# A low-pass filter between two channel projections: images unrolled, first and second matmuls side by side, the corner term moved to VectorE

## The reference

```python
xs = jnp.einsum('bhwc,dc->bhwd', x, W1) + b1      # x: (16, 64, 64, 768) f32, W1: (192, 768)
xs = jax.nn.gelu(xs, approximate=False)
xs = fft_low(xs)       # per image and channel: keep the 32 x 32 low frequencies of the 64 x 64 FFT, then abs()
xs = jnp.einsum('bhwd,cd->bhwc', xs, W2) + b2     # back to 768 channels
return x + xs
```

## Time and profile before

| | |
|---|---|
| median of 3 runs | 2668.43 us (2667.24 to 2670.11) |
| profiled execution, span from the first to the last instruction | 2680.7 us |
| own time of the profiled execution | not listed; its span stands 12.3 us (0.46%) over the median |
| mean granted TensorE clock | 0.975 of full speed |
| TensorE busy | 95% |
| DMA, mean of 16 engines | 59.8% of the span, 509 MB |

### The profile page before, as it was taken

The page is one execution under the profiler, slowest core; times in us unless marked ns, Lnnn a source line. Parts: engine busy times, 40 slices in busy tenths (PEclk is TensorE's granted clock), DMA queues, the critical chain, the costliest instruction groups (busy, mean ns, idle before and its releaser), DMA issues.

```text
span 2680.7 us, 53277 instructions
## 1 busy us (share of the span) xinstructions
PE 2549.4 (95%) x16864; PEld 2485.4 (93%) x16864; DVE 1833.9 (68%) x3980; ACT 1350.4 (50%) x3077; POOL 397.9 (15%) x500
## 2 busy tenths in 40 slices
PE   8899898998999989899998999989999899998999
PEld 7799898998989989899898999989999899998999
DVE  6487575775758757587675766757667576675767
ACT  5355454554545545455454545545455454554544
POOL 1102021020211202112020120201202012020120
PEclk9899999999999999999999999999999999999999
DMA  6474664746647466474665846558455584555845
GB/s 207 106 252 138 201 242 114 264 129 200 240 114 261 131 198 242 114 273 129 204 230 129 282 116 215 208 135 298 103 211 202 140 300 99 207 204 145 299 102 221
DMA packets 342566, 509.48 MB, mean 190 GB/s; under 512 B 78418, under 2 KB 210770, under 8 KB 342228
## 3 DMA queue, kind: packets, MB, share of 16 engines
q1 hardware_dynamic: 342228, 505.31, 59.8%
HBM read 253.60 MB, written 251.66 MB: 188 GB/s over the span
## 4 chain that ended last, share of the span: by engine, by line
PE 83%; DMA 6%; SPq 4%; issue 3%; DVE 2%; ACT 2%; DVEq 0%; ACTq 0%
PE ps L400 22%; PE ps L385 12%; PE ps L401 10%; PE ps L472 6%; PE ps L462 6%; PE ps L463 5%; PE ps L469 5%; PE ps L466 5%; DMA xt_hi<-filtered_rows 4%; PE ps L437 3%; SPq L317 2%; PE ps L411 2%; PE ps L445 2%; DMA filtered_rows<-filt 2%; PE ps L413 2%
## 5 line engine op out<-in xcount | busy, mean ns | idle before, releaser
L400 PE MATMUL ps<-w1s,xt_hi 128*128 128x384 f32 x3072 | 980.2, 374 | 0.0
L521 ACT ACTIVATE xt_hi<-ps 128x512 fp32r<-128x512 f32 x768 | 457.7, 598 | 697.8 <-PE ps L385 674.5
L401 PE MATMUL ps<-w1s,xt_lo 128*128 128x192 f32 x3072 | 772.3, 251 | 0.0
L640 DVE TENSOR_TENSOR xt_lo<-ps,xt_hi 128x512 fp32r<-128x512 f32 x768 | 529.8, 691 | 282.4 <-ACT xt_hi L521 279.6
L702 DVE TENSOR_TENSOR xs<-ps,xs 128x384 f32<-128x384 f32 x1024 | 564.5, 556 | 210.9 <-PE ps L472 159.8
L401 PEld LDWEIGHTS ps<-w1s,xt_lo 128*128 128x128 f32 x3072 | 588.0, 191 | 0.0
L400 PEld LDWEIGHTS ps<-w1s,xt_hi 128*128 128x128 f32 x3072 | 578.8, 188 | 0.0
L472 PE MATMUL ps<-w2b_hi,ob 128*128 128x384 f32 x1024 | 357.0, 349 | 42.7 <-DVE ob L693 42.7
L763 POOL TENSOR_TENSOR diff<-hid 128x192 f32<-128x192 f32 x240 | 232.2, 967 | 1016.8 <-ACT hid L529 1016.8
L462 PE MATMUL ps<-w2a_hi,oa_hi 128*128 128x384 f32 x1024 | 361.3, 353 | 20.8 <-DVE xs L702 19.7
L385 PE MATMUL ps<-ident,xs 128*128 128x128 f32 x2304 | 344.1, 273 | 11.2 <-DMA xs<-x_dram 10.6
(11 more groups left out here) (62 smaller groups left out, 3051.3 us busy)
## 6 DMA issues: line engine op xcount, KB each, us to landing
out_dram<-xs SPq DMA_DIRECT2D x127, 1536.0 KB, 9.3
xs<-x_dram SPq DMA_DIRECT2D x80, 1536.0 KB, 7.2
filtered_rows<-filt SPq DMA_DIRECT2D x256, 192.0 KB, 2.0
x_tail<-x_dram SPq DMA_DIRECT2D x32, 1536.0 KB, 8.5
xs<-x_dram SPq DMA_DIRECT2D x32, 768.0 KB, 6.3
xt_hi<-filtered_rows SPq DMA_DIRECT2D x64, 256.0 KB, 5.1
cols_b<-filtered_rows SPq DMA_DIRECT2D x128, 128.0 KB, 5.4
xt_lo<-filtered_rows SPq DMA_DIRECT2D x64, 256.0 KB, 6.4
```

The lines of the kernel that those rows point to most:

```text
L400: nc.tensor.matmul(ps_h[t % 2][:, 0:2 * D], hi, w1s[:, k, :], start=k == 0, stop=False)
L401: ins = nc.tensor.matmul(ps_h[t % 2][:, D:2 * D], lo, w1s[:, k, 0:D], start=False, stop=k == KC - 1)
L521: nc.scalar.activation(xt_hi[:, n % XT_SLOTS, :], ps_xt[n % 2][:], ACT.Copy).then_inc(s_xhi, 1)
L640: nc.vector.tensor_tensor(xt_lo[:, n % XT_SLOTS, :], ps_xt[n % 2][:], xt_hi[:, n % XT_SLOTS, :].bitcast(F32), ALU.subtract).then_inc(s_xlo, 1)
```

## The change

The image loop is gone: all 256 pairs (ALL) of the 16 images are unrolled in one list of steps. Step s has first matmuls of pair s and second matmuls of pair s - 17 (LAG = 17). The filter along H of image i stands in step 16 i + 17, after the first unit of that step, so one step after `filter_w_pair` of the image's last pair. In that step the four halves of the second matmuls come at the end.

`xs` becomes 18 slots of a pair. Three of four pairs are kept in 16 slots from their transposes to their store. Every fourth pair is loaded once for the transposes and once more for the addition (`load_again`), each into one slot of its own. Loads and stores are of one pair (768 KB) instead of four tiles. The copy by ScalarE (565) goes.

`filtered_rows` becomes two tensors, `rows_a` (128 channels) and `rows_b` (64), each pair written with two DMAs. They are read back in five groups of four DMAs as pairs become ready: pairs 0 to 3, 4 to 7, 8 to 11, 12 to 14, and pair 15 alone. A group of n pairs goes to 4 n partitions for each half of W, with contiguous runs of 16 KB or 8 KB. `cols_a` has its own memory.

The corner is no longer 12 matmuls. `corner_values` makes 64 columns with two small float32 matmuls, VectorE copies them (`corner_copy`), and adds them while it stores each of the 12 banks (`y_group`), so that VectorE stores all 12. ScalarE then takes the absolute value in place (`y_group_positive`). The banks rotate over four (`ps_y`). Identity and W1 are loaded by ScalarE's queue.

```diff
-LAG = 8
+LAG = PAIRS + 1
+READS = [(0, 4), (4, 4), (8, 4), (12, 3), (15, 1)]
...
+            def write_rows(p):
+                i, q = divmod(p, PAIRS)
+                sp.wait_ge(s_fs, p + 1)
+                if q == 0 and i > 0:
+                    sp.wait_ge(s_cols, 16 * READ_DMAS * i)
+                sp.dma_start(rows_in[0][:, 2 * q:2 * q + 2, :], filt[:, p % 2, :, 0:P]).then_inc(s_rw[p % 2], 16)
+                sp.dma_start(rows_in[1][:, 2 * q:2 * q + 2, :], filt[:, p % 2, :, P:D]).then_inc(s_rw[p % 2], 16)
+            def read_rows(i, n):
+                first, number = READS[n]
+                end = i * PAIRS + first + number
+                sp.wait_ge(s_rw[0], 32 * ((end + 1) // 2))
+                sp.wait_ge(s_rw[1], 32 * (end // 2))
...
+                h = slice(4 * first, 4 * (first + number))
                 for w2 in range(2):
+                    sp.dma_start(cols_a[w2 * H + h.start:w2 * H + h.stop, :, :],
+                                 rows_a[h, w2 * W2:(w2 + 1) * W2, :]).then_inc(s_cols, 16)
+                    sp.dma_start(cols_b[w2 * H + h.start:w2 * H + h.stop, :, :].rearrange("p m n -> p (m n)"),
+                                 rows_b[h, w2 * W2:(w2 + 1) * W2, :].rearrange("h w d -> h (w d)")).then_inc(s_cols, 16)
...
+            for s in range(STEPS + 1):
+                if s + 2 < ALL:
+                    load_first(s + 2)
+                if 0 <= s - LAG - 1 < ALL - 1:
+                    store(s - LAG - 1)
+                if 1 <= s <= ALL:
+                    i, q = divmod(s - 1, PAIRS)
+                    for n, (first, number) in enumerate(READS):
+                        if first + number == q:
+                            read_rows(i, n)
+                    write_rows(s - 1)
+                    if q == PAIRS - 1:
+                        read_rows(i, len(READS) - 1)
+                p = s - LAG + 2
+                if 0 <= p < ALL and again(p):
+                    load_again(p)
...
+            def corner_values(i):
+                pe.wait_ge(s_twice, i + 1)
+                pe.wait_ge(s_fs, PAIRS * (i + 1))
+                nc.tensor.matmul(ps_f[:, 2 * D:2 * D + 32], corner_acc[:, 0:P], kmat[:], start=True, stop=True)
+                nc.tensor.matmul(ps_f[:, 2 * D + 32:2 * D + 64], corner_acc[:, P:2 * P], kmat[:], start=True, stop=True).then_inc(s_cmm, 1)
+            def filter_h(i):
+                pe.wait_ge(s_cols, 16 * READ_DMAS * (i + 1))
+                pe.wait_ge(s_add, HALVES * i)
+                for g in range(GROUPS):
...
+                    if g == 3:
+                        pe.wait_ge(s_corner, i + 1)
+                    elif g >= 4:
+                        pe.wait_ge(s_yev, GROUPS * i + g - 3)
                     for m in range(4):
...
+                        ins = nc.tensor.matmul(bank[:, m * P:(m + 1) * P], data, fh[:], start=True, stop=True)
                     ins.then_inc(s_y, 1)
...
+            for s in range(STEPS):            # TensorE
+                i, r = y_image(s), second_pair(s)
+                for j in range(UPP):
+                    if UPP * s + j + AHEAD < UNITS:
+                        transpose_unit(UPP * s + j + AHEAD)
+                    if s < ALL:
+                        mm1_unit(UPP * s + j)
+                    if j == 0 and i is not None:
+                        corner_values(i)
+                        filter_h(i)
+                    if j == 1 and 1 <= s <= ALL:
+                        filter_w_pair(s - 1)
+                    if r is not None and i is None:
+                        for u in OUT_HALVES[j]:
+                            out_half(r, u)
+                if i is not None:
+                    for u in range(4):
+                        out_half(r, u)
...
+            def y_group(i, g):                # VectorE
...
+                fix = corner[:, g % 3 // 2, :].rearrange("p (n m) -> p n m", m=4).unsqueeze(1).to_broadcast([P, 16, 8, 4])
+                nc.vector.tensor_tensor(y_of_group(g).rearrange("p (r n) m -> p r n m", n=8),
+                                        ps_y[g % 4][:].rearrange("p (m r n) -> p r n m", m=4, n=8), fix,
+                                        ALU.add).then_inc(s_yev, 1)
...
+            def y_group_positive(i, g):       # ScalarE
+                act.wait_ge(s_yev, GROUPS * i + g + 1)
+                y = y_of_group(g)
+                nc.scalar.activation(y, y, ACT.Abs).then_inc(s_yab, 1)
```

More of the change, by code:

```diff
@@ L353, in _, with load_first @@
-            turns(sp, turn)
-            for g in range(MAIN_GROUPS):
-                sp.wait_ge(s_out[g], 16 * IMAGES)
-            sp.wait_ge(s_tail_out, 16 * (TAIL_GROUPS * IMAGES + GROUP - 1) + 1)
-            for n in range(2):
-                sp.wait_ge(s_fw[n], 16 * PAIRS // 2 * IMAGES)
+            def load_first(p):
+                slot = slot_first(p)
+                if again(p) and nth_use(p) > 1:
+                    sp.wait_ge(s_t, UPP * (p - 4) + UPP)
+                elif not again(p) and nth_use(p) > 1:
+                    sp.wait_ge(s_st[slot], 16 * (nth_use(p) - 1))
+                elif slot in (12, 13, 14):
+                    sp.wait_ge(s_setup, SET_UP)
+                if p == 0:
+                    sp.dma_start(xs[:, 0:1, :], x_v[:, 0:1, :]).then_inc(s_x_first, 16)
+                    sp.dma_start(xs[:, 1:2, :], x_v[:, 1:2, :]).then_inc(s_ld[0], 16)
+                else:
+                    sp.dma_start(x_pair(slot), x_v[:, 2 * p:2 * p + 2, :]).then_inc(s_ld[slot], 16)
@@ L361, in _ @@
+            store_last_pair()
+            for slot in range(SLOTS):
+                stored = sum(16 for p in range(ALL) if slot_second(p) == slot)
+                if slot == slot_second(ALL - 1):
+                    stored += 16
+                if stored:
+                    sp.wait_ge(s_st[slot], stored)
         @block.tensor
@@ new lines, in _ @@
+            for n in range(AHEAD):
+                transpose_unit(n)
+            for s in range(STEPS):
[16 more added lines that the diff above has]
+                        out_half(r, u)
@@ L593, in _ @@
-            turns(act, turn)
+            for n in range(AHEAD):
+                xt_hi_unit(n)
+            for s in range(STEPS):
+                i, r = y_image(s), second_pair(s)
+                for j in range(UPP):
+                    if UPP * s + j + AHEAD < UNITS:
+                        xt_hi_unit(UPP * s + j + AHEAD)
+                    if j == 0 and 1 <= s <= ALL:
+                        gelu_pair(s - 1)
+                    if j == 0 and i is not None:
+                        for g in range(GROUPS):
+                            y_group_positive(i, g)
+                        split_hi_pair(r)
+                    if j == 2 and 1 <= s <= ALL:
+                        stage_filtered(s - 1)
+                    if r is not None and j == (0 if i is None else 2) and r + 1 < ALL and not image_starts(r + 1):
+                        split_hi_pair(r + 1)
+                    if j == 2 and s in (2, 3):
+                        set_up_hi(s - 2)
@@ L610, in set_up_filters @@
             def set_up_filters():
[L611 to L612 removed]
+                dve.wait_ge(s_const, 16 * CONSTANTS)
                 link(nc.vector.tensor_copy(fw_hi[:], fwf))
@@ L745, in _ @@
-            turns(dve, turn)
+                slot = slot_second(p)
+                dve.wait_ge(s_o, n + 1)
+                if u == 0 and again(p):
+                    dve.wait_ge(s_ld[AGAIN_C], 16 * nth_use(p))
+                x_half = xs[:, 2 * slot + t, f * HALF:(f + 1) * HALF]
+                nc.vector.tensor_tensor(x_half, ps_o[n % 3][:, 0:HALF], x_half, ALU.add).then_inc(s_add, 1)
+            set_up_at = {0: set_up_filters, 1: set_up_w2, 4: set_up_w2a_lo, 5: set_up_w2b_lo,
+                         6: set_up_b2_hi, 7: set_up_b2_lo, 8: set_up_b2_lo_rest}
```

709 lines of the change are left out of this document (262 added, 447 removed).

## The result

The changed kernel takes 2768.9 us (median of 4 runs, 2762.3 to 2771.4) beside 2667.8 us for the kernel before on the same chip: a ratio of 1.037 (95% interval 1.034 to 1.040), slower by 3.7%. I had forecast 2612 us and a range that ended at 2675 us. The profiled execution has a span of 2764.6 us at a mean granted clock of 0.951.

A forecast was written before the change was run, and what follows sets the result against it. TensorE, busy for 95% of the span, was taken as the bound. Terms 2247.7 + 158.4 + 148.8 + 24 + 33.5 + 12 gave 2624.4 us of span, 2612 us at the median; range 2535 to 2675 us.

The forecast's parts named there:

- Side by side everywhere: First and second matmuls paired in all steps: 256 pairs at 8.78 us, 2247.7 us, with every fourth pair's second load hidden.
- The wait for the reads: TensorE waits ahead of the filter along H for the last filtered rows: 9.05 us per image, 148.8 us in all.
- The rival on the other side: Read rate goes by partition count: wait of 18 us, 2756 us, 3.3% slower; chance 0.12 for waits above 12 us.
- The corner: Filter along H: twelve 0.32 us matmuls per image go, banks take 0.80 us at TensorE's pace; 158.4 us in all.
- the account against before: Changes from the old span: corner -61, old stalls and slow clock -198, new wait, clock and stall +206, start and end -7.
- The slow clock: After the wait for reads, the filter's first two banks run at the lower clock: 1.5 us per image, 24 us.
- After the filter: Second matmuls start without a wait, then the fourth half stalls 1.9 us on VectorE's first addition; 33.5 us in all.
- The old gap of 3.46 us on "issue": TensorE's gap where the image loop turns, said to go in 15 turns with the slow clock behind it.
- Start and end: Span beyond the 16 image periods: 19.1 us before, 12 us taken for the changed kernel.
- quick reads of 3 us: Rival in which the last reads wait only 3 us without loss of clock: 2504 us; quick reads had chance 0.20.

The follow-up runs named there:

- Experiment 2: The changed kernel with pairs 12 to 15 read back as one group behind the last write: 2671.06 us, ratio 0.999 to the kernel before.
- experiment 3: The changed kernel with last read groups of pairs 12, 13 and pairs 14, 15: 2709.54 us, ratio 1.015 to the kernel before.
- experiment 4: The kernel before without its 12 corner matmuls per image, the correction left out of the output: 2671.97 us, ratio 1.002.

## Why the prediction was wrong, by its steps

**Side by side everywhere: right.** 8.78 to 8.80 us per step, the second load hidden; the only waits for x, 7.9 us in five places, stand ahead of the first filter.

**The wait for the reads: the step that failed.** I had 148.8 us and the trace shows 236.8, or 14.8 us per image instead of 9.05. Two things were in it. The reads begin where I had put them only if the write lands in 2.0 us; it took 8.3 us, because I priced the second write's landing by its median and not behind the narrow reads issued 1.6 us before it. I had written down, beside the Trainium skill's rule, that these reads would hold the last write up, and left it out of the sum. The read itself took 8.9 us, at the long end of my bounds of 3.0 to 10.3. The hold is partly covered by TensorE's 2.9 us of work after the write: 8.3 + 8.9 - 2.9 = 14.3, the 14.24 of the trace (in the mean of the images 8.5 + 9.1 - 2.7 = 14.8). Of the excess of 5.75 us per image the hold is nearly the whole, 8.3 against the 2.4 us that I had. Experiment 2, with a hold of 2.5 us, has a wait of 8.6 us: my term with its own assumption.

**The rival on the other side** named the right cause, partitions, and the wrong law. It had a rate in proportion to their number, a wait of 18 us and 2756 us. The measured read is far shorter than 16 + 2 us; the wait is long because two narrow reads follow each other. Its deciding point, a wait of 12.6 us, was too high, since the other terms of the sum were low as well: experiment 2, with 8.6 us, is level with the kernel before, and experiment 3, with 10.7 us, is 1.5% slower. Even the wait that I forecast, 9.05 us, would have left no gain. A chance of 0.12 was too small for a mechanism that the rows of half-speed reads pointed to.

**The corner: mis-sized.** I took a bank to be 0.80 us and the corner matmul 0.32, from the starts of records. The sum of 1.12 was right and the cut between them was not: banks stand 0.89 us apart, so the corner was 0.23. The banks cost 16 x (12 x 0.893 + 0.3) = 176.3 us instead of 158.4. VectorE's 0.69 us was exact, and never the pace. Its 1.12 us come from rows of the kernel before, and the 0.89 from all the banks of the later kernels. And the account against before counted a gain of 61 us that the kernel before did not hold (experiment 4); with the 0.3 us of the new corner matmuls it should have been 56 in any case.

**The slow clock: low.** The filter of image 6 took 13.25 us, 2.5 us more than 12 x 0.893, where I had 1.5 for two banks. The first two took 3.57 us by their starts and the third 1.64, so three were slow. 16 times make 40 us instead of 24.

**After the filter: right, a little high.** 1.38 us instead of 1.9, at the fourth half and for the addition, as described. With 2.5 us for the last image's split the term is 23 us instead of 33.5. The old gap of 3.46 us on "issue" is gone.

**Start and end: low.** What is left of the span is 2764.6 - 2247.7 - 176.3 - 236.8 - 40 - 23.1 = 40.7 us, not 12. Of it 23 us are idle time of TensorE, 19.9 ahead of the first filter: 7.9 for loads of x, 6.1 for the first low part, 4.4 for the identity, 1.5 for a low part of the hidden sums. The other 17 us are busy time beyond my prices, 5 of them the 0.02 us by which a step is over 8.78; the rest I can't place.

Together: the wait +88, banks +18, clock +16, stall -10, start and end +29, 141 us over the sum of 2624.4. The wait with the clock behind it is three quarters. One number among the rivals is off too: the 2504 us for quick reads of 3 us were not brought to the median; they are 2492.

## What to carry to other kernels

A last transfer on the critical path is priced from its issue to its landing behind what is already in flight, not by the median of its kind; ask what the DMAs issued just before it go to. Splitting a read by image rows so that a piece lands on four neighbouring partitions made it no shorter than one four times its size: give the pieces partitions far apart and put the permutation into a constant matrix. And work that runs under a wait (the corner's matmuls here) was no gain when it was removed; look for the waits around such work before you price it.

## What the runs showed of the hardware that I had not expected

- A read of 192, 384 or 768 KB to 4, 8 or 16 neighbouring partitions of each half took 8.9, 9.0 and 8.5 us; spread over every fourth partition, 192 KB took 5.4 us, though each issue rose from 0.3 to 0.6 us.
- A write of 192 KB from 128 partitions to DRAM, which lands in 2.0 us alone, took about 8 us when it was issued within 2 us of narrow reads on the same queue, though it goes the other way. A quarter of its parts landed in 2.2 us, the other three quarters together with the last of the reads, which had been issued to 12 partitions in 12 parts each.
- TensorE came out of a wait of 1.89 us at the clock level of 2.4 GHz (granted clock 1.00), and after one of 14.24 us was at 0.50 for its first 3.5 us and slow for three banks. With the waits cut from 14.8 to 2.3 us an image, the mean granted clock rose from 0.951 to 0.993.
